# Four graph layers on one core: first-layer loads, masks and shifts rearranged, and head preparation done in halves of the tiles

## The reference

```python
# layer 0
h = max(layernorm(x), 0)
Wh1 = h @ W @ a[:512];  Wh2 = h @ W @ a[512:]
e = leaky_relu(Wh1 + Wh2.T, 0.2)
att = softmax(where(adj > 0, e, -1e12), axis=1)
neg = -softmax(where(adj > 0, -e, -1e12), axis=1)
x = x + elu(concat([att @ h, neg @ h]) @ wtrans)
# layer 1, 8 heads of 64 columns
nX = a_ln * (n - mean(n)) / (std(n) + eps) + b_ln      # n: a head's columns of h @ W
s  = leaky_relu(at1 + at2.T, 0.2) * adj                # at1, at2: nX times two vectors
y  = softmax(where(adj, s, -32768)) @ nX + nX
x = x + elu(y)
```

## Time and profile before

| | |
|---|---|
| median of three runs | 2878.79 us |
| the profiled execution | 2878.06 us, its span 2876.3 us |
| TensorE busy | 2531.2 us, 88% of the span |
| VectorE busy | 1992.8 us, 69% |
| ScalarE busy | 1699.8 us, 59% |
| GpSimd busy | 123.7 us, 4% |
| granted TensorE clock, mean | 0.95 |

### The profile page before, as it was taken

How to read it: one execution, slowest core, us unless ns; L and a number is a source line. 1 busy time by engine, 2 the same in 40 slices (tenths; PEclk the granted TensorE clock), 3 DMA queues, 4 the chain that set the end, 5 groups by cost and what they waited for, 6 DMA issues and landing times. The chain is left out here.

```text
span 2876.3 us, 54791 instructions
## 1 busy us (share of the span) xinstructions
PE 2531.2 (88%) x20921; PEld 1562.1 (54%) x20921; DVE 1992.8 (69%) x3608; ACT 1699.8 (59%) x3096; POOL 123.7 (4%) x73
## 2 busy tenths in 40 slices
PE   6938999999997559999999996759994979999999
PEld 3513444444443328888888885324443745555554
DVE  4738899999995768988998986542226633445674
ACT  2317888888885348788878785751112334444452
POOL 2730000000000000000000000000000000000000
PEclk9978999999999779999999998879996989999999
DMA  3023433433431344111111113403224223444451
GB/s 125 0 103 120 148 135 132 155 128 125 139 129 65 115 150 171 36 38 36 27 36 36 36 28 134 153 1 103 89 86 180 95 84 101 115 118 119 128 133 49
DMA packets 193038, 280.57 MB, mean 98 GB/s; under 512 B 95669, under 2 KB 123429, under 8 KB 187065
## 3 DMA queue, kind: packets, MB, share of 16 engines
q1 hardware_dynamic: 186489, 246.00, 26.6%
q10 hardware_dynamic: 6336, 31.72, 3.5%
HBM read 208.89 MB, written 68.80 MB: 97 GB/s over the span
## 5 line engine op out<-in xcount | busy, mean ns | idle before, releaser
L1395 PE MATMUL m_acc<-m_y,m_b 128*128 128x260 f16 x3872 | 662.5, 276 | 51.1 <-DVE m_b L1222 35.2
L1398 PE MATMUL m_acc<-m_y,m_at 128*128 128x130 f16 x3872 | 660.1, 221 | 0.0
L1191 ACT ACTIVATE m_above<-m_u,m_nvs 128x512 bf16<-128x512 f32 (+1 forms) x864 | 521.6, 682 | 93.1 <-DVE m_b L1222 92.0
L1395 PEld LDWEIGHTS m_acc<-m_y,m_b 128*128 128x128 f16 x3872 | 376.6, 97 | 115.4 <-issue 34.8
L804 PE MATMUL m_acc<-keep_z_hi,m_p_hi 128*128 128x512 f16 x968 | 365.9, 378 | 58.1 <-DVE m_p_lo L659 55.1
L1398 PEld LDWEIGHTS m_acc<-m_y,m_at 128*128 128x128 f16 x3872 | 381.2, 98 | 0.0
L805 PE MATMUL m_acc<-keep_z_lo,m_p_hi 128*128 128x512 f16 x968 | 366.4, 378 | 0.0
L808 PE MATMUL m_acc<-keep_z_hi,m_p_lo 128*128 128x512 f16 x968 | 365.3, 377 | 0.0
L1222 DVE TENSOR_TENSOR m_b<-m_above,m_at 128x1024 f16<-128x1024 bf16 (+1 forms) x432 | 278.4, 653 | 69.5 <-PE m_acc L1398 38.5
L1738 PE MATMUL m_hi<-keep_xs_hi,keep_at_first 128*128 128x512 f16 x484 | 182.8, 378 | 40.1 <-SPq L1719 32.5
L559 ACT ACTIVATE m_p_hi<-m_pm 128x512 f16<-128x512 f32 x242 | 150.9, 624 | 88.2 <-DVE m_pm L652 80.5
(11 more groups left out here) (293 smaller groups left out, 4957.7 us busy)
## 6 DMA issues: line engine op xcount, KB each, us to landing
m_a_rows<-adj ACTq DMA_DIRECT2D x44, 704.0 KB, 4.2
...
m_at<-at SPq DMA_DIRECT2D x5, 2816.0 KB, 19.1
...
p_x_all<-x SPq DMA_DIRECT2D x6, 1536.0 KB, 14.7
...
```

Source lines behind the costliest of these rows:

```text
L1191: act.activation(pair(above, a % RA, nb)[:, i], u[:, g % RU, 0:nb], ACT.Relu, bias=nvs[:, k, 2 * p + i:2 * p + i + 1], scale=STEEP).then_i ...
L1395: pe.matmul(full.rearrange("p l y e -> p (l y e)"), pair(b01, (m // 2) % RB, nb)[:, m % 2, q // 2, half], y12[:, k % 2, j].rearrange("p l ...
L1398: last = pe.matmul(full[:, :, 1, :], at[:, i0 + q // 2, j, half], y2[:, k % 2, j], start=False, stop=(j == T - 1), skip_group_check=True)
```

## The change

prep0: the weights stand as two halves of 4 x 512 columns with a semaphore each. ScalarE makes the high part of a half (before its steps -3 and -2), VectorE the low part (before -3 and -1); the columns of W @ a have tiles of their own and are split on VectorE before step -1. TensorE waits, in tile 0, for a half's low part ahead of that half's products. `a_rows` and `am` belong to both stages: SP loads the first four pieces of `adj` in prep0 (the last two behind the masks of the first two), and ScalarE masks pieces 0 and 1 before its steps 10 and 12. The column-sum product and its copy leave prep0; zsum is kept.

attention0: ScalarE issues no load at the start, and does an exponential on a few values first. SP no longer waits for piece 1 and has no spread(0). TensorE does the column sum of zsum into `acc`; VectorE takes the means from there between the extremes of pieces 1 and 2. For block 0 VectorE copies g broadcast along 128 columns into `o`, TensorE transposes it in four blocks, and VectorE copies the result to `g_row`.

attention1: the head columns come in two loads, ahead of aln and bln, and every step of a head's preparation works on 11 tiles. The first half stands in blocks 1 to 3, the second in blocks 3 and 4. mean, add_shift and add_mean come in the head's own blocks 0 and 1 (`complete`). For head 0, only the first half up to the negation, and normalise and stretch of the second, stand before the first pair; the rest is between the pairs of block 0. TensorE waits for the second half's negation at j = 11.

```diff
--- before.py
+++ after.py
@@ prep0
-        NX = 2 * D + 2
-        w = kit.sb("w", [KC, NX])
-        w_hi, w_lo = kit.sb("w_hi", [KC, NX], F16), kit.sb("w_lo", [KC, NX], F16)
+        w = kit.sb("w", [2, KC, D])
+        w_hi, w_lo = kit.sb("w_hi", [2, KC, D], F16), kit.sb("w_lo", [2, KC, D], F16)
...
+                        sp.dma_start(w[:, c], dram["wtr0"][c * D:(c + 1) * D, :].rearrange("(k p) n -> p k n", p=P)).then_inc(w_in[c], 16)
+                for c in range(4):
+                    if c >= 2:
+                        sp.wait_ge(am_made, c - 1)
+                    sp.dma_start(a_rows[:, c % 2, :], dram["adj"][(c // 2) * P:(c // 2 + 1) * P, (c % 2) * HN:(c % 2 + 1) * HN]).then_inc(
+                        piece_in[c % 2], 16)
...
+                for piece in piece_in:
+                    sp.wait_ge(piece, 32)
...
+                def weights(c):
+
+                    act.wait_ge(w_in[c], 16)
+                    act.activation(w_hi[:, c], w[:, c], ACT.Copy, scale=WS).then_inc(w_hi_made, 1)
+
+                def mask_rows(c):
+
+                    act.wait_ge(piece_in[c], 16)
+                    act.activation(am[:, c, :], a_rows[:, c, :], ACT.Copy, scale=BIG, bias=-BIG).then_inc(am_made, 1)
...
-                pipeline(act, (2, high), (4, lambda t, b: root(act, t, b, std, s)), (3, normalise), (0, finish))
+                pipeline(act, (2, high), (4, lambda t, b: root(act, t, b, std, s)), (3, normalise), (0, finish),
+                         before=[(-3, lambda: weights(0)), (-2, lambda: weights(1))] + [(10 + 2 * c, lambda c=c: mask_rows(c)) for c in range(2)])
 
...
+                        if isinstance(t, int) and t == 0:
+                            pe.wait_ge(w_lo_made, half + 1)
...
-                pe.wait_ge(zsum_made, 2 * T)
-                for half in range(2):
-                    of = slice(half * D, (half + 1) * D)
-                    last = pe.matmul(main[:, 0, of], ones32[:], zsum[:, of], start=True, stop=True, skip_group_check=True)
-                last.then_inc(cs_ready, 1)
...
+                def rest(c):
+
+                    dve.wait_ge(w_hi_made, c + 1)
+                    dve.scalar_tensor_tensor(w_lo[:, c], w[:, c], WS, w_hi[:, c], ALU.mult, ALU.subtract).then_inc(w_lo_made, 1)
+
+                def weights_a():
+
                     dve.wait_ge(wa_made, 1)
-                    dve.tensor_copy(w[:, :, 2 * D:NX], small[:, 0, 0:2 * KC].rearrange("p (m s) -> p m s", s=2)).then_inc(wa_copied, 1)
+                    dve.tensor_copy(wa[:], small[:, 0, 0:2 * KC].rearrange("p (m s) -> p m s", s=2)).then_inc(wa_copied, 1)
                     dve.wait_ge(wa_copied, 1)
...
-                         before=[(-4, weights)] + [(t0 - 6, lambda c=c: here(c)) for c, (t0, n) in enumerate(CHUNKS)])
+                         before=[(-3, lambda: rest(0)), (-1, lambda: rest(1)), (-1, weights_a)] + [(t0 - 6, lambda c=c: here(c)) for c, (t0, n) in enumerate(CHUNKS)])
                 dve.wait_ge(uvt_ready, 1)
                 dve.tensor_copy(uvT[0:2 * T, :], tp[0:2 * T, 0, 0, :]).then_inc(uvt_copied, 1)
-                dve.wait_ge(cs_ready, 1)
-                dve.tensor_copy(cs[:], main[:, 0, :]).then_inc(used, 1)
...
@@ attention0
-                    sp.wait_ge(g_out, 16 * (ib + 1))
+                    sp.wait_ge(g_out, 16 * ib)
...
-                sp.wait_ge(piece_in[1], 16)
                 load_u(0)
                 load_mask(0, 0)
-                spread(0)
                 load_mask(0, 1)
...
-                load(0)
-                load(1)
+                act.sem_inc(am_made, 2)
                 act.wait_ge(set_up, 1)
                 act.wait_ge(v_made, 3)
-                for c in range(4):
+                act.activation(den[:, 0, :], sign[:, 0, :], ACT.Exp)
+                for c in (2, 3):
                     mask_rows(c)
                     load(c + 2)
...
+                    if m == 0:
+                        dve.wait_ge(g_first, 1)
+                    elif j == 0:
+                        dve.wait_ge(g_in[ib % 2], 16 * ((ib + 1) // 2))
...
+                def column_means():
+
+                    dve.wait_ge(zs_made, 1)
+                    dve.tensor_scalar(cd[:], acc[:, 2, 1], 1.0 / N, None, ALU.mult).then_inc(cd_made, 1)
+                    dve.wait_ge(cd_made, 1)
+                    dve.scalar_tensor_tensor(cd[:], acc[:, 2, 0], 1.0 / N, cd[:], ALU.mult, ALU.subtract).then_inc(cd_made, 1)
+
+                def spread_first():
+
+                    wide = o[:, 0, :].rearrange("p (s q c) -> p s q c", s=2, q=2)
+                    dve.wait_ge(ext_link, 6)
+                    dve.tensor_copy(wide, g[:].unsqueeze(3).broadcast_to([P, 2, 2, P])).then_inc(wide_made, 1)
+                    dve.wait_ge(turned, 1)
+                    dve.tensor_copy(g_row[:, 0].rearrange("p s i -> p (s i)"), acc[:, 2, 0]).then_inc(g_first, 1)
+
                 for c in range(4):
                     for least in (False, True):
                         extreme(c, least)
+                    if c == 1:
+                        column_means()
                 shifts(0)
+                spread_first()
                 scores(0)
...
+                pe.wait_ge(ones_made, 1)
+                for s in range(2):
+                    last = pe.matmul(acc[:, 2, s], ones32[:], zsum[:, s * D:(s + 1) * D], start=True, stop=True, skip_group_check=True)
+                last.then_inc(zs_made, 1)
+                pe.wait_ge(wide_made, 1)
+                pe.wait_ge(cd_made, 2)
+                for i in range(4):
+                    last = pe.transpose(acc[:, 2, 0, i * P:(i + 1) * P], o[:, 0, i * P:(i + 1) * P], keep["ident"][:])
+                last.then_inc(turned, 1)
...
@@ attention1
+                    src = dram["c1"].rearrange("(t p) (k e) -> k p t e", p=P, e=DH)[k]
+                    for hf in range(2):
+                        sp.dma_start(c[:, k % 2, part(hf), 0:DH], src[:, part(hf), :]).then_inc(c_in[2 * (k % 2) + hf], 16)
...
+                load_c(0)
                 sp.dma_start(aln[:], dram["aln"].broadcast_to([P, DH])).then_inc(ln_in, 16)
                 sp.dma_start(bln[:], dram["bln"].broadcast_to([P, DH])).then_inc(ln_in, 16)
-                load_c(0)
...
-                split(0, 0)
-                split(0, 1)
+                split(0, 0, 0)
+                split(0, 1, 0)
...
-                        if k + 1 < H and (n, p) in ((2, 8), (4, 1)):
-                            split(k + 1, 0 if n == 2 else 1)
+                        if k + 1 < H and (n, p) in SPLIT_AT:
+                            split(k + 1, *SPLIT_AT[n, p])
+                        if g == 0 and p in (2, 3):
+                            split(0, p - 2, 1)
                 low(ALL - 1)
...
+        SPLIT_AT = {(2, 4): (0, 0), (3, 0): (1, 0), (3, 10): (0, 1), (4, 5): (1, 1)}
...
+                def weigh(k, n, hf):
+
+                    dve.wait_ge(chat_made, 2 * k + hf + 1)
                     if n == 1:
-                        dve.wait_ge(ylo_made, 2 * k + 1)
+                        dve.wait_ge(ylo_made, turn(k, 0, hf))
                     elif k > 0:
-                        dve.wait_ge(c_made, k)
-                    dve.tensor_tensor(yf[:], c[:, k % 2], over_tiles((d1, d2)[n][:, k, :], YW), ALU.mult).then_inc(yf_made, 1)
...
+                def negate(k, hf):
+
+                    dve.wait_ge(ylo_made, turn(k, 1, hf))
+                    for l in range(2):
+                        last = dve.tensor_scalar(y12[:, k % 2, part(hf), l, 1, :], y2[:, k % 2, part(hf), l, :], -1.0, None, ALU.mult)
+                    last.then_inc(neg_made, 1)
+
+                def sum_half(k, hf):
+                    dve.wait_ge(chat_made, 2 * k + hf + 1)
+                    dve.tensor_reduce(csp[:, hf, :], c[:, k % 2, part(hf), 0:DH].rearrange("p t e -> p e t"), AXX, ALU.add).then_inc(half_made, 1)
 
                 def sum_head(k):
-                    dve.wait_ge(chat_made, k + 1)
+                    dve.wait_ge(half_made, 2 * k + 2)
                     if k > 0:
                         dve.wait_ge(cs_made, k)
-                    dve.tensor_reduce(csp[:], c[:, k % 2, :, 0:DH].rearrange("p t e -> p e t"), AXX, ALU.add).then_inc(csp_made, 1)
-
...
                 def prepare(k, n, p):
 
-                    if (n, p) == (1, 9):
-                        normalise(k)
-                    if (n, p) == (2, 0):
-                        stretch(k)
-                    if (n, p) == (2, 2):
-                        weigh(k, 0)
-                    if (n, p) == (2, 9):
+                    for hf, steps in enumerate((((1, 9), (2, 0), (2, 2), (2, 7), (2, 9), (3, 3), (3, 5)),
+                                                ((3, 0), (3, 1), (3, 8), (4, 1), (4, 3), (4, 8), (4, 10)))):
+                        if (n, p) == steps[0]:
+                            normalise(k, hf)
+                        if (n, p) == steps[1]:
+                            stretch(k, hf)
+                        if (n, p) == steps[2]:
```

(79 more changed lines are left out.)

156 lines of the change are left out of this document (81 added, 75 removed).

## The result

The changed kernel takes 2813.26 us (median of four runs, 2810.47 to 2813.64) against 2878.76 for the kernel before beside it: a ratio of 0.977 with an interval of 0.975 to 0.979. The forecast was 2812 in a range of 2800 to 2832. The profiled execution took 2813.64 with a span of 2811.8, so the two profiled spans differ by 64.5 us.

What follows compares the result with a forecast made beforehand. TensorE, busy 88% of the span, was taken as the bound, with idle time at stage starts and in attention1's heads. Gains of 8.0 + 5.0 + 18.0 + 1.3 + 10.5 + 24.5 = 67.3 us gave 2812, range 2800 to 2832.

Steps and rivals of the forecast that it cites:

- Start of prep0: prep0's first product at 24.8 instead of 32.75, with weights in two halves: 8.0 us gained, bounds 6.5 and 9.
- End of prep0: The barrier directly follows GpSimd's last addition, at 173.64 instead of 178.63: 5.0 us gained.
- a stage which begins earlier ends earlier by as much: Steady parts of prep0 and attention0 are untouched, so an earlier start moves the stage's end equally.
- Start of attention0: v_row's load alone in front and shifts by TensorE transposes instead of DMAs: 18.0 us gained.
- rival A: At attention0's start v_row shares bandwidth with the masks: 7 us slower, 2819 us; chance 0.10.
- The table load: At attention0's start the exp table (1.28 us) is loaded early: 1.3 us gained.
- Start of attention1: Fewer preparation steps ahead of b: first product 11.3 us earlier, 10.5 gained after waits in block 0; bounds 7 and 12.
- the halving: Half-width preparation steps in attention1: thirteen more instructions a head, estimated 2.0 us a head more, overlap leaving half.
- Heads: attention1's heads 1 to 7: of a 4 us stall in block 5, 0.5 stays; 3.5 x 7 = 24.5 us gained.
- Rival B: VectorE's lead doesn't cover attention1's blocks 3 and 4; 2 to 4 us a head remain, 2826 or 2836; chance 0.20.
- Rival C: In attention1 VectorE and ScalarE wait in turn and VectorE becomes the bound: 2880 us and over; chance 0.03.
- The sum: Gains over the whole kernel: 8.0 + 5.0 + 18.0 + 1.3 + 10.5 + 24.5 = 67.3 us.

## Why the prediction was right, step by step

**Start of prep0: right**, 24.35 for 24.8. ScalarE's half took 1.91 (estimate 2.0) and started at 14.13 (14.3), x landed for 16.84 (17.0). Undoing the split alone brought 33.02 back.

**End of prep0: right; 1.7 us short in the profiled execution alone.** The barrier follows the addition by 0.98, so that 4.9 of the 5.0 are there. The last addition ends only 6.8 us earlier, 165.96 for 172.73, after a start 8.4 earlier. But in the same kernel executed again it ends at 164.44 and the whole stretch to v_row's issue gains 5.0, as forecast; in the nine other profiles with this end of prep0 the stretch takes 140.3 to 141.9 us. So that a stage which begins earlier ends earlier by as much holds here within what executions differ by, about 2 us.

Of the 1.6 us by which the profiled execution fell short before the last addition, 1.0 lie between first product and first scores: 7.51 us before, 8.55 after, 7.43 in the same kernel again. TensorE's clock makes most of this. Timelines, the last product that takes over 0.5 us and the first at its later length: the changed kernel, then the same executed again.

```profile
28.61 0.63 PE L158 MATMUL p_main<-p_w_lo,p_hT_hi 128*128 128x512 f16 x1
...
29.31 0.38 PE L157 MATMUL p_main<-p_w_hi,p_hT_hi 128*128 128x512 f16 x1
```

```profile
26.67 0.57 PE L159 MATMUL p_main<-p_w_hi,p_hT_lo 128*128 128x512 f16 x1
27.07 0.38 PE L157 MATMUL p_main<-p_w_hi,p_hT_hi 128*128 128x512 f16 x1
```

Products of 512 columns take 0.63 us and follow one another by 0.43, later 0.38 and 0.21; in the first 3.1 us of attention0, where the granted clock is 0.50 (1.2 GHz), they take up to 0.63 as well. Eleven take over 0.5 us in the profiled execution, six in the same kernel again and eight in the kernel before. Five more at 0.21 us each are 1.1, the whole difference between the two executions; three more are 0.6 of the 1.0 against the kernel before. In both executions the scores also come 0.4 us later behind their products than before; I can name no cause for that.

The other 0.6 are the tiles, 125.9 for 125.3 (and 125.3 in the same kernel again). That GpSimd's additions cost the tiles time at all is shown: 124.1 in the one profile without them, 124.7 to 125.9 in the thirteen profiles with them, and L113 at 0.16 instead of 1.27 us. In the profiled execution L113 starts inside an addition 16 times of 20 (1.54 us in the mean then), in the kernel before 14 times of 22 (1.42), and executed again the mean of all is 1.14; why they meet as often as they do was not settled. The addition of the last tile stood on the path too: dropping it was worth 3.3 us of the barrier, and I had not looked for it.

**Start of attention0: right**, 18.5 for 18.0. v_row was there 6.5 after the barrier (6.3), the steps by TensorE took 2.33 (2.75; the wide copy was 0.43, not 0.65), and the chance of 7 us for shared queues (rival A) is refuted by the run that held the masks back: 0.47. The table load stands at 167.40 under v_row's flight: 1.4 for 1.3.

**Start of attention1: right**, with errors in it that cancel. 11.4 us were gained at the first product, where I had worked out 11.3. VectorE's row of half steps took 8.08 us for the 7.2 forecast (a half step is 0.89 alone, and 0.82 in a row for the 0.80 taken; a half split is 0.82 for 0.75), and it began 6.4 us after the stage's start for 7.4; neither counts, since the mask lands 1.1 us behind the row. From the 11.3 I had taken off 0.8 for waits in block 0. Block 0 takes 0.9 us longer than before, so the size is right, but the reason differs between executions. Windows of 18 us from the first product, the changed kernel and then the same executed again:

```profile
1040.78:1058.78 18.00, 17.97 (x179) 15.61 (x180) 17.34 (x26) 13.97 (x23) 1.09 (x1) 0.85 0.98 351
```

```profile
1041.09:1059.09 18.00, 17.15 (x179) 14.73 (x180) 17.34 (x26) 14.18 (x23) 1.10 (x1) 0.91 1.00 359
```

In the first TensorE hardly waits and loses its time to the clock: 0.85 in the mean is about 5.5 us at the lower level (4.1 in the kernel before). In the second the clock rises after 3.1 us, TensorE waits for 0.85, and the block takes 17.75 us all the same. VectorE is busy for 17.34 of 18 us in both, which suggests that its work sets the length of this block; no run changes it to show that. The Trainium skill's figure for an instruction (VectorE: DVE Perf Modes, the TRN2 errata, (704 + 151) / 0.96 = 891 ns) agrees with the 0.89; the 2.0 us a head that I had estimated from it for the halving do not show: VectorE's busy time rose by 0.9.

**Heads: the sum right, both of its terms wrong.** I put the stall at 4 us, from a pace without it of 81.6, and left 0.5 of it. The pace without a stall is 82.2: from its first product to its last, the last head of the kernel before takes 82.15. The 712 records in 60 us of the earlier trace rows count products that lie across the edges, which makes a head too short by 0.6 us. The stall was 3.5 (block 5 took 11.2 us, and 7.66 in that last head), and of it 0.1 stayed (7.75). So 24.1 for 24.5 is two errors that cancel, which is luck. Rival B (the stall moves to blocks 3 and 4) is refuted: these take 14.9 us each before and after, also with the moved whole steps, whose pieces are twice as long, and with a pair less in the ring. Rival C needed VectorE at its limit; it is busy 80.1 of 85.

**What I had wrong about why** is the halving. I costed it as part of what frees the heads; it is worth nothing there and costs 0.9 us of VectorE's time. Its gain is at attention1's start, where a whole preparation stood on the path: up to 6.5 us at the first product, with the loads' share in it not separated, of which block 0 takes 1.5 back.

**The sum.** 67.3 were forecast, 67.1 are in the table and 64.5 in the spans. Of the 2.6 between them, 2.4 lie where nothing was edited (prep1 and layers 2 and 3), and the 0.9 of attention1's block 0 and the 0.7 gained in attention0 nearly cancel. The same kernel's runs lie 3.2 us apart, so this can't be told from the spread of executions.
